# Softplus of the time steps: five operations or one activation

## The reference, cut to what matters

```python
hidden = jax.nn.silu(x + conv_bias[None, :, None])
hs_ble = hidden.transpose(0, 2, 1)
ssm_p = jnp.einsum('ble,ed->bld', hs_ble, W_x)
dt, Bm, Cm = jnp.split(ssm_p, [TR, TR + N], axis=-1)
dts = jax.nn.softplus(jnp.einsum('blr,re->ble', dt, W_dt) + b_dt)
dA = jnp.exp(dts[..., None] * A[None, None])
dBu = dts[..., None] * Bm[:, :, None, :] * hs_ble[..., None]
# state = dA * state + dBu over the 512 time steps, y = sum over N of state * C
```

## Time and profile before

| | |
|---|---|
| median of 3 runs | 1209.81 us (1209.77 to 1210.84) |
| the profiled execution, its own time | 1212.85 us |
| its span, first to last instruction | 1211.1 us |
| mean granted TensorE clock | 0.856 |
| busy: VectorE | 974.8 us (80%) |
| busy: TensorE | 866.9 us (72%) |
| busy: ScalarE | 855.8 us (71%) |
| busy: GpSimd | 814.6 us (67%) |

### The profile page before, as it was taken

The page is one execution under the profiler, slowest core; times in us unless marked ns, Lnnn a source line. Parts: engine busy times, 40 slices in busy tenths (PEclk is TensorE's granted clock), DMA queues, the critical chain, the costliest instruction groups (busy, mean ns, idle before and its releaser), DMA issues.

```text
span 1211.1 us, 10560 instructions
## 1 busy us (share of the span) xinstructions
PE 866.9 (72%) x2718; PEld 339.3 (28%) x2718; DVE 974.8 (80%) x783; ACT 855.8 (71%) x1458; POOL 814.6 (67%) x515
## 2 busy tenths in 40 slices
PE   7933488878368789877549788896727946675995
PEld 2221133322023233332114233332202312222331
DVE  2459999987789987778888977887788999999733
ACT  2386777766557887786666886878756788787546
POOL 2238888876667776686767766868766777777533
PEclk9966699988679889988869899998977978778996
DMA  5184444442973334242793332443395353225100
GB/s 172 35 183 113 97 113 113 126 112 55 244 196 74 87 97 112 70 122 74 186 271 91 85 97 73 103 117 92 89 249 165 72 140 87 59 70 156 27 0 35
DMA packets 66684, 135.03 MB, mean 111 GB/s; under 512 B 13120, under 2 KB 19392, under 8 KB 66624
## 3 DMA queue, kind: packets, MB, share of 16 engines
q1 hardware_dynamic: 65904, 134.28, 43.5%
q10 hardware_dynamic: 720, 0.08, 0.0%
HBM read 62.75 MB, written 4.46 MB: 55 GB/s over the span
## 4 chain that ended last, share of the span: by engine, by line
PE 27%; issue 24%; ACT 18%; DVE 18%; DMA 5%; POOL 4%; SPq 2%; DVEq 0%; ACTq 0%; POOLq 0%
PE dense L919 18%; DVE st L817 12%; PE dense L974 6%; ACT dA L598 5%; POOL st L466 3%; DMA rep<-steps 2%; DVE dBu L811 2%; PE dense L951 2%; DMA wide<-w_out 1%; ACT squares L629 1%; DVE hs L795 1%; SPq L358 1%; ACT du_rep L606 1%; ACT tb L588 1%; PE dBu L929 1%
## 5 line engine op out<-in xcount | busy, mean ns | idle before, releaser
L466 POOL TENSOR_TENSOR st<-st,Cb 128x1024 f32<-128x1024 f32 x250 | 584.4, 2359 | 180.9 <-DVE st L817 153.5
L817 DVE TENSOR_TENSOR_SCAN st<-dA,dBu 128x1024 f32<-128x1024 f32 x256 | 570.2, 2269 | 0.3 <-ACT dA L598 0.3
L598 ACT ACTIVATE dA<-rep,Aneg 128x511 f32<-128x511 f32 x512 | 327.7, 710 | 82.0 <-DMA rep<-steps 51.6
L811 DVE TENSOR_TENSOR dBu<-du_rep,Bb 128x1024 f32<-128x1024 f32 x250 | 294.6, 1224 | 91.8 <-ACT du_rep L606 60.6
L919 PE MATMUL dense<-xTs,Win 128*128 128x512 f32 x512 | 242.2, 618 | 16.6 <-DMA xTs<-xT 7.7
L919 PE MATMUL dense<-wide,hs 128*128 128x512 f32 x256 | 122.2, 634 | 57.9 <-DVE hs L795 34.3
L919 PEld LDWEIGHTS dense<-xTs,Win 128*128 128x128 f32 x512 | 99.1, 198 | 154.2 <-issue 153.5
L974 PE MATMUL dense<-pj,Win 128*128 128x512 f32 (+1 forms) x192 | 106.1, 704 | 47.0 <-DVEq L798 21.2
L951 PE MATMUL dense<-st,sel 128*32 128x512 f32 x1024 | 124.3, 629 | 2.9 <-POOL st L466 2.9
L606 ACT COPY du_rep<-rep 128x512 f32<-128x512 f32 x128 | 74.4, 581 | 41.2 <-DVE dBu L811 39.4
L945 PE MATMUL dense<-hs,Ddiag 128*128 128x512 f32 x64 | 41.2, 731 | 81.9 <-ACT Ddiag L676 72.2
(11 more groups left out here) (117 smaller groups left out, 998.4 us busy)
## 6 DMA issues: line engine op xcount, KB each, us to landing
rep<-steps SPq DMA_DIRECT2D x512, 128.0 KB, 2.7
Win<-w_in SPq DMA_DIRECT2D x64, 256.0 KB, 2.7
wide<-w_out SPq DMA_DIRECT2D x4, 2048.0 KB, 14.0
Win<-w_conv SPq DMA_DIRECT2D x24, 256.0 KB, 2.7
wide<-bc_rows SPq DMA_DIRECT2D x24, 256.0 KB, 6.5
xTs<-xT SPq DMA_DIRECT2D x4, 1024.0 KB, 10.9
Bb<-bc_rows SPq DMA_DIRECT2D x16, 256.0 KB, 10.8
Cb<-bc_rows SPq DMA_DIRECT2D x16, 256.0 KB, 11.8
```

The lines of the kernel that those rows point to most:

```text
L466: nc.gpsimd.tensor_tensor(s, s, C[:, j, :], ALU.mult).then_inc(s_p, 1)
L598: nc.scalar.activation(dA[:, u % 2, j, 1:T], rep[:, u % REPS, 0, 1:T], ACT.Exp, scale=Aneg[:, u % UNITS, j:j + 1]).then_inc(s_dA, 1)
L811: V.tensor_tensor(dBu[:, j, :], du_rep[:].unsqueeze(1).to_broadcast([P, JH, T]), B[:, j, :], ALU.mult).then_inc(s_mul, 1)
L817: V.tensor_tensor_scan(st[:, u % RING, j, :].rearrange("p j t -> p (j t)"), dA[:, u % 2, j, :].rearrange("p j t -> p (j t)"), dBu[:, j, :] ...
```

## The change

`soft` becomes one activation, Softplus, from PSUM with the bias, straight into `steps`. Abs, Relu, Exp, Ln and GpSimd's addition go, and with them the semaphore `s_zw` and the use of the ring of intermediate tiles by `z`. Since ScalarE now writes `steps` itself, it waits for that tile's last readers (the `exps` of block n - 3, `s_dA`, and GpSimd's product of block n - 3, `s_du`); the bank is freed after Softplus is done. GpSimd keeps its multiplication by `hs`.

```diff
-    temp_keys = [key for key in order if key[0] in "zgc" or key[0] == "h" and key[1] == 0]
+    temp_keys = [key for key in order if key[0] in "gc" or key[0] == "h" and key[1] == 0]
...
-                        pool.wait_ge(s_zw, 3 * (n + 1))
-                        if n >= 3:
-
-                            pool.wait_ge(s_dA, NJ * NQ * (n - 2))
-                        nc.gpsimd.tensor_tensor(steps[:, n % 3, 0, :], t, a, ALU.add).then_inc(s_dt, 1)
                         pool.wait_ge(s_dt, n + 1)
                         nc.gpsimd.tensor_tensor(steps[:, n % 3, 1, :], steps[:, n % 3, 0, :], hs[:, kb % 2, i, :],
                                                 ALU.mult).then_inc(s_du, 1)
-                        pool.sem_inc(s_temp, 1)
...
+                n = NE * b + e
                 ps, free = full(("z", b, e))
-                a, t = temp_slot(("z", b, e))
-                n = 3 * (NE * b + e)
-                nc.scalar.activation(t, ps, ACT.Abs, bias=bdt[:, e:e + 1]).then_inc(s_zw, 1)
-                nc.scalar.activation(a, ps, ACT.Relu, bias=bdt[:, e:e + 1]).then_inc(free, 1)
-                act.wait_ge(s_zw, n + 1)
-                nc.scalar.activation(t, t, ACT.Exp, scale=-1.0).then_inc(s_zw, 1)
-                act.wait_ge(s_zw, n + 2)
-                nc.scalar.activation(t, t, ACT.Ln, bias=ones[:, 0:1]).then_inc(s_zw, 1)
+                if n >= 3:
+                    act.wait_ge(s_dA, NJ * NQ * (n - 2))
+                    act.wait_ge(s_du, n - 2)
+                nc.scalar.activation(steps[:, n % 3, 0, :], ps, ACT.Softplus, bias=bdt[:, e:e + 1]).then_inc(s_dt, 1)
+                act.wait_ge(s_dt, n + 1)
+                act.sem_inc(free, 1)
```

More of the change, by code:

```diff
@@ L248, in decoder_layer @@
         s_cc = sem("c_spread")
-        s_zw = sem("softplus_step")
         s_dt = sem("steps_ready")
```

## The result

| | before | after |
|---|---|---|
| median of 4 runs each | 1210.32 us (1209.77 to 1211.04) | 1179.14 us (1173.03 to 1180.63) |
| profiled execution / its span | 1212.85 / 1211.1 us | 1180.63 / 1178.8 us |
| granted clock, mean | 0.856 | 0.863 |

The ratio is 0.9733, with a 95% interval of 0.9697 to 0.9768: 31 us faster. The forecast was 1179.0.

The account below looks back on a forecast made before the run. No single engine set the time: VectorE led, while ScalarE, held up in `soft`, kept TensorE and VectorE waiting. Terms summed to 32.1 us, giving 1177.7 at the median's level; with 1.3 given back, 1179.0, range 1171 to 1187 (wider: 1165 to 1195).

Parts of the forecast that it names:

- The price of one `soft`: ScalarE's time for each of 32 `soft`: 5.11 us down to about 3.3, 1.8 less, with one table load each way.
- The hidden load: First two `soft`, ahead of the scan: Softplus's load lies under the wait for `z`; gain 3.0 us, without that 1.8.
- Item 0: Four `soft` with convolution: `pj` is copied earlier, TensorE and VectorE idle less; 1.5 us each, 6.0 in all.
- The later four of items 1 and 2: TensorE, nearly full, waits less for work behind `soft`: 5.1 us in item 1, 6.3 in item 2, sum 11.4.
- The ends: Three `soft` at the ends of items 0 to 2: copy of `bc_s` comes earlier; 1.8 us each, 5.4 in all.
- the first steps: Three `soft` at the first step of items 1 to 3: transfers of B, C and W_out set what follows; gain 0.
- half-handed-back rival: Inside and at ends of items, gains only move engines to their next wait, half worth: 1194 us; chance 0.13.
- The bank that is freed later: Last `soft`, at 1083: Softplus behind its load frees the bank later than Relu did, TensorE waits; loss 0.7 us.
- One set for all: Rival for every `soft`: Softplus shares a table set with Tanh and Exp, no loads left: 1164 us; chance 0.10.
- the dear Softplus: Rival: Softplus itself takes over 2.5 us; at 3.4 us, 1226 us; chance 0.07 together with another loss.
- the 1.3 us given back: Added to the forecast time because most terms are the most a wait can give: 1177.7 to 1179.0 us.

Follow-up runs that it names:

- without its own wait: Changed kernel, but Softplus frees the bank itself, GpSimd waits for that signal and ScalarE doesn't wait for its own Softplus; ratio 0.9712 to the kernel before.
- with the GpSimd pass: Changed kernel with one GpSimd pass over the tile (multiplying by one) put back between Softplus and the product with hs; ratio 0.9716 to the kernel before.
- third-load kernel: Changed kernel with a tiny Ln (128x1) behind each Softplus, forcing a third table load into each `soft`; ratio 0.9948 to the kernel before.
- late pairs: Changed kernel with two `z` made in the first step of every second block, one block ahead of use, sharing loads; ratio 1.0044 to the kernel before.

## Why the prediction was right, and by how much each step

**The price of one `soft`.** Forecast 5.11 to 3.3 us, measured 3.44; the 0.14 are the wait for Softplus's own end, which the forecast had costed at nothing beside the load. 63 loads, 0.69 us for Softplus, as forecast. ScalarE's busy time fell by 56, not 66 us: I had added the durations of Abs, Relu and Exp, though Abs and Relu overlap by 0.1 us each with the next and Abs with what stands before it, where the path (1.67 x 32 = 53, and two loads) was the better guide. It was a remark and no term of the sum.

**The hidden load.** The rows after, answering to the earlier trace rows:

```profile
57.11 1.28 ACT L578 ACT_TABLE_LOAD   x1
59.21 0.69 ACT L578 ACTIVATE steps<-dense,bdt 128x512 f32<-128x512 f32 x1 [0.81 <-PE dense L911]
60.02 0.58 ACT L718 COPY small<-dBu 32x512 f32<-32x512 f32 x1
...
72.55 0.59 ACT L598 COPY du_rep<-rep 128x512 f32<-128x512 f32 x1 [6.91 <-DMA rep<-steps]
```

The load ran at 57.11, ahead of the product, and the copy came 2.95 us earlier, 3.0 by the forecast. The first `du_rep` came only 2.2 earlier, because the transfers behind it took longer. In the second profile of the same kernel it came at 68.67, with `dt_s` already copied at 54.05 instead of 56.51, before any changed instruction. So the class has a spread of 4 us between executions of one kernel, and its gain can't be sized better than that.

**The places inside the items.** This is where the sum agrees and its parts don't. Item 0 gave 5.4 to 6.3 for 6.0, but not 1.5 in each step: 0.5, 0.1, 1.5 and 3.3. The later four of items 1 and 2 gave 15.3 for 11.4. The rows put the difference into the length of TensorE's bursts. Some of the eight-matmul bursts of `c` in item 0; before:

```profile
241.43 5.36 PE L974 MATMUL dense<-pj,Win 128*128 128x512 f32 x8 [3.43 <-DVEq L798]
...
252.31 5.36 PE L974 MATMUL dense<-pj,Win 128*128 128x512 f32 x8 [2.09 <-issue]
```

and after:

```profile
178.04 6.66 PE L966 MATMUL dense<-pj,Win 128*128 128x512 f32 x8 [3.43 <-DVEq L790]
...
237.09 3.66 PE L966 MATMUL dense<-pj,Win 128*128 128x512 f32 x8 [3.43 <-DVEq L790]
...
246.40 3.66 PE L966 MATMUL dense<-pj,Win 128*128 128x512 f32 x8 [2.22 <-issue]
```

The same burst behind the same 3.43 us pause takes 3.66, 5.36 or 6.66 us. The windows (the clock stands behind the five busy times) show the granted clock for it. After, for 178 to 184 and 237 to 241:

```profile
178.00:181.00 3.00, 2.96 (x4) 1.44 (x5) 2.92 (x3) 1.09 (x3) 1.83 (x1) 0.50 0.02 4
181.00:184.00 3.00, 3.00 (x4) 1.08 (x4) 3.00 (x2) 2.81 (x5) 1.29 (x1) 0.50 0.00 0
...
237.00:241.00 4.00, 3.92 (x9) 1.82 (x10) 3.88 (x3) 2.08 (x5) 1.88 (x1) 1.00 0.65 164
```

0.50 is the 1.2 GHz level, 1.00 the 2.4 GHz level. In the step at 178 the low level lasted longer than before (there, 5.29 us for the burst), and ate 1.4 of the 1.5 us that `pj` gave, which is why VectorE's wait stood at 2.34. In the changed kernel's second profile the burst at this place took 5.16 us, about as before, and the block gave its 1.6. At 237 and 246 the low level didn't come at all: the second burst starts 9.31 us behind the first instead of 10.88, and is itself 1.70 shorter, 3.3 together. In item 1, before and after:

```profile
493.85 0.63 PE L937 MATMUL dense<-ident,small 128*128 128x128 f32 x4 [3.29 <-ACT ta L574]
494.94 5.22 PE L974 MATMUL dense<-pj,Win 128*128 128x512 f32 x8 [0.46 <-ACT pj L566]
```

```profile
478.08 0.63 PE L929 MATMUL dense<-ident,small 128*128 128x128 f32 x4 [1.72 <-ACT ta L567]
479.17 3.66 PE L966 MATMUL dense<-pj,Win 128*128 128x512 f32 x8 [0.46 <-ACT pj L559]
```

The clock's mean was 0.72 before and 1.00 after:

```profile
494.00:500.00 6.00, 5.54 (x13) 2.52 (x13) 2.77 (x4) 6.00 (x11) 6.00 (x4) 0.72 0.06 13
```

```profile
479.00:483.00 4.00, 3.83 (x9) 1.82 (x10) 3.46 (x5) 4.00 (x8) 4.00 (x3) 1.00 0.33 71
```

The pause fell by 1.57 us, near the forecast, and the burst behind it by another 1.56. The block gave 3.1, not 1.8. The whole excess of the eight blocks sits in four of them, 12, 13, 20 and 21: they gave 10.8 us for 7.2, and the second burst of `c` in each fell from 5.22, 6.21, 4.92 and 6.07 us to 3.66, 5.36, 3.66 and 5.28, 4.5 us in sum. The other four gave 4.5 for 4.2. That is the mis-sized term: the forecast took a wait's length for its price, and put at nothing what happens to the burst behind a shorter pause. It repeats: the eight blocks gave 16.0, 15.6 and 14.7 us in the profiles of the changed kernel again, without its own wait, and with the GpSimd pass.

TensorE's 13 us less of busy time over the whole span are no measure of this. The `c` bursts account for 4.9 us of them (106.1 to 101.2 us in sum). The kernel without its own wait has the same 101.2, yet a TensorE busy for 865.0 us and a mean clock of 0.854, and its span is shorter still, 1175.5 us. No kernel here changed the clock alone, so its share in the total was read from bursts and not isolated by a run.

**The item boundaries.** The ends gave 7.7 for 5.4, the first steps -3.1 for 0. TensorE's three waits for the copy of `bc_s` fell from 15.9 to 11.5 us in sum, 1.5 each and not 1.8; in the first of them the two matmuls behind the wait also took 1.04 instead of 1.92 us. The kernels without its own wait and with the GpSimd pass gave 5.0 and 4.9 us in this class, so of the 2.3 above the forecast most is no fixed gain. The forecast put the first steps at nothing because transfers set them; they do, and they don't move as far as the work before them. VectorE's waits for B there were 16.0 us in total and are 17.8; TensorE, which waited once for W_out (18.1 us) and otherwise for `finish`, waits all three times for the transfer:

```profile
PE dense L911 <- DMA wide<-w_out: 53.9, 3, 18.2
...
DVE dBu L803 <- DMA Bb<-bc_rows: 17.8, 3, 6.4
```

This is the half-handed-back rival, right in its mechanism and at its place, but 3 us large and not 15.

**The bank that is freed later.** TensorE waits 4.39 us for it in the last `soft`, against 3.49, 0.9 more where 0.7 were forecast; the class lost 1.4.

**The rivals.** One set for all and the dear Softplus fell with the rows of ScalarE. The third-load kernel is what a dear `soft` looks like: 1.46 us more of hold is 26 to 31 us more of time.

The hit within 0.2 us is partly luck: the same kernel gave 1176.8 in a later series, its profile 38.8 us instead of 32.3, the 1.3 us given back came from no row, and errors of +3.9, +2.3, -3.1, -0.8, -0.7, -0.6, -0.6 and -0.2 cancelled in the sum.

## What to carry to other kernels

Price an edit of an in-order queue by how long it holds what stands behind it, table loads included, at each place where it stands, and not by its busy time: 40 us less of GpSimd were worth nothing, 53 us less of holds 31 to 38, and the next 40 us of loads nothing that could be measured, in item 0 because a block can't fall below what its fullest engine needs. When work is moved in a shared turn of buffers, look first at who gets the buffer next; that cost 7 us here, and over 30 in the late pairs together with steps that came late. Where TensorE pauses, a wait's length is not its whole price: the burst behind it ranged from 3.66 to 6.66 us here.

## What was not expected of the hardware

- The burst behind an unchanged pause of 3.43 us ran at the high clock level, at the low one, or partly at each: 3.66, 5.19 and 6.66 us for eight matmuls of 128x512 float32, in one execution. What decides it was not settled.
- Two profiled executions of the same kernel differ by 6.5 us of span (1178.8 and 1172.3), of which 3.9 arise ahead of the first unit, in transfers and at TensorE (four matmuls ahead of `dt_s` took 3.72 us in one and 2.10 in the other).
- A table load directly behind an activation starts 0.01 us after its end; with a wait for that activation's signal between them it is 0.16 us.
- A GpSimd multiplication of 128x512 float32 by a broadcast column takes 1.05 us, by a full tile 1.27.
